# Three all-head attention stages: scores once with the mask added by VectorE, exponentials turned by TensorE, and VectorE's copies four banks behind its maxima

## What is computed

```
logits = q @ k.T * scale           # per head, 256 x 256
att    = softmax(where(mask, logits, -inf))
x      = x + (att @ v) @ Wo.T      # L3x: x + relu(...)
```

## Time and profile before

| | |
|---|---|
| median of 3 runs | 1761.01 us |
| profiled execution, its own time | 1761.7 us |
| its span | 1760.0 us |
| mean granted TensorE clock | 0.908 |
| busy: TensorE, VectorE, ScalarE, GpSimd | 1415.8, 875.7, 756.1, 430.4 us |
| L0a: start, 192 banks of exponentials, end | 29.1, 66.8 to 405.7, 415.6 us |
| L2a: start, 96 banks, end | 951.6, 992.2 to 1152.7, 1161.8 us |
| L3x: 128 banks | 1417 to 1625 us |

### The profile page before, as it was taken

How to read it: one execution, slowest core, us unless ns; L and a number is a source line. 1 busy time by engine, 2 the same in 40 slices (tenths; PEclk the granted TensorE clock), 3 DMA queues, 4 the chain that set the end, 5 groups by cost and what they waited for, 6 DMA issues and landing times. The chain is left out here.

```text
span 1760.0 us, 27583 instructions
## 1 busy us (share of the span) xinstructions
PE 1415.8 (80%) x10001; PEld 785.2 (45%) x10001; DVE 875.7 (50%) x2460; ACT 756.1 (43%) x1609; POOL 430.4 (24%) x513
## 2 busy tenths in 40 slices
PE   6899999997899999885997899976083577787585
PEld 4344444444544444463455344455062434444364
DVE  4555555542355555455213565447223657666433
ACT  3244443443177777451440133443020467776233
POOL 4533333310121110100001444201544042210134
PEclk9999999998999999895999999987586889999687
DMA  7900000000000000000003100000122000000022
GB/s 209 133 1 1 2 1 1 1 1 0 1 1 1 1 1 1 1 1 1 1 1 127 51 1 1 1 1 10 51 80 78 1 19 13 7 13 1 7 59 77
DMA packets 60255, 42.31 MB, mean 24 GB/s; under 512 B 13189, under 2 KB 54121, under 8 KB 60121
## 3 DMA queue, kind: packets, MB, share of 16 engines
q1 hardware_dynamic: 54752, 32.42, 7.7%
q0 software_dynamic: 3552, 7.33, 1.2%
q10 hardware_dynamic: 1816, 0.81, 0.2%
HBM read 25.88 MB, written 14.66 MB: 23 GB/s over the span
## 5 line engine op out<-in xcount | busy, mean ns | idle before, releaser
L885 ACT ACTIVATE L0a_probs<-L0a_psL 128x512 f32<-128x512 f32 x192 | 104.2, 594 | 202.0 <-PE L0a_psL L693 73.5
L1262 ACT ACTIVATE L3x_e<-L3x_e,L3x_neg_max 128x256 f32<-128x256 f32 x256 | 112.4, 499 | 55.8 <-DVE L3x_neg_max L1314 55.2
L949 DVE TENSOR_REDUCE L0a_mx_part<-L0a_psS 128x4 f32<-128x512 f32 x120 | 77.3, 686 | 105.6 <-PE L0a_psS L636 81.3
L1182 PE MATMUL L3x_psE<-ident,L3x_e 128*128 128x128 f32 x512 | 84.3, 297 | 38.6 <-ACT L3x_e L1262 25.1
L1314 DVE CUSTOM_DVE_ANT_0 L3x_e<-L3x_psS,L3x_mask_rows 128x256 f32<-128x256 f32 x256 | 93.5, 420 | 31.2 <-PE L3x_psS L1174 30.9
L538 POOL TENSOR_SCALAR L0a_km<-L0a_kT,quad_rows 128x256 f32<-128x256 f32 x64 | 58.4, 930 | 199.3 <-ACT L0a_kT L856 199.3
L628 PE MATMUL L0a_psS<-L0a_km,L0a_qT 32*128 32x512 f32 x360 | 101.4, 640 | 0.2 <-DVE L0a_mx_part L954 0.2
L885 ACT ACTIVATE L2a_probs<-L2a_psL 128x512 f32<-128x512 f32 x96 | 52.1, 595 | 107.3 <-PE L2a_psL L689 72.5
L1182 PEld LDWEIGHTS L3x_psE<-ident,L3x_e 128*128 128x128 f32 x512 | 58.6, 149 | 87.2 <-ACT L3x_e L1262 68.3
L662 PE MATMUL L0a_psL<-L0a_qm,L0a_kT 32*128 32x512 f32 x256 | 72.1, 637 | 21.8 <-DVE L0a_mx L949 20.3
L1516 PE MATMUL L1a_psL<-L1a_soft_near,neg_tri 128*128 128x512 f32 x128 | 67.9, 612 | 0.2 <-DVE L1a_soft_near L1723 0.2
(11 more groups left out here) (719 smaller groups left out, 3476.4 us busy)
## 6 DMA issues: line engine op xcount, KB each, us to landing
L2f_rows<-packed_rows SPq DMA_DIRECT2D x8, 325.0 KB
packed_rows<-zeros SPq DMA_DIRECT2D x1, 2560.0 KB, 32.4
experts_L_L<-in_L_ffn_w_dram SPq DMA_DIRECT2D x1, 2048.0 KB, 8.9
unpacked_rows<-zeros SPq DMA_DIRECT2D x1, 2048.0 KB, 22.5
scores_L_experts_L<-in_L_ffn_w_dram SPq DMA_DIRECT2D x1, 2048.0 KB, 8.0
L2f_back_rows<-unpacked_rows SPq DMA_DIRECT2D x16, 128.0 KB, 2.6
L3x_mask_rows<-in_mask_Bx1xSxS_ff_dram SPq DMA_DIRECT2D x8, 256.0 KB, 2.7
sorted_rows<-zeros SPq DMA_DIRECT2D x1, 1472.0 KB, 20.1
```

Source lines behind the costliest of these rows:

```text
L885: nc.scalar.activation(probs[:, half, a, k, :], psL[i % RING][:], ACT.Exp, scale=scale).then_inc(s_prob, 1)
L949: nc.vector.tensor_reduce(dst, psS[a][:].rearrange("p (j n) -> p j n", j=4), AX.X, ALU.max).then_inc(s_red, 1)
L1182: last = nc.tensor.transpose(psE[i % 2][:, c * P:(c + 1) * P], e[:, i % RING, c * P:(c + 1) * P], mem.ident[:])
L1262: last = nc.scalar.activation(at, at, ACT.Exp, bias=neg[:, i % RING, j:j + 1], scale=-1.0)
```

## The change

In `quad_heads` the second pass goes away: scores are computed once, with the query rows on the partitions, and handled as `masked_heads` handles them. `qm`, the maxima's way through TensorE, `shift`, `hide` and both mask matmuls are gone. `reduce` adds the mask (`causal_rows` is new, built by GpSimd in the prologue) and writes minima and shifted scores; in group 0 a bank has 4 pieces of 128 columns, in groups 1 and 2 it has 2 of 256. `exponent` has as many pieces. The projections' copies, the copy of `raw` and the norm change engines: `keep_h` and `keep_raw` go to VectorE, `next_h` and `divide` to GpSimd. In both functions `score` of the next group stands one bank earlier in TensorE's queue (r == 1), and VectorE's `keep` of a bank stands four banks behind its `reduce`; `settle_x` of batch b stands at the first bank of b + 2. In `masked_heads` ScalarE's `invert` and `keep_h` move by one bank.

```diff
 def quad_heads(...):
-                def variants(src, dst, b, done):
...
+                def next_h(b):
+                    if b == 0:
+                        pool.wait_ge(scales, 2)
+                    else:
+                        pool.wait_ge(s_turn, b)
...
+                next_h(0)
+                next_h(1)
                 nc.gpsimd.memset(v[:], 0.0).then_inc(consts, 1)
...
                 for b in range(NB):
+                    if b + 2 < NB:
+                        if rope:
+                            combine(b + 2)
+                        variants(b + 2)
+                    if biased:
+                        add_bias(b)
+                    if b > 0:
+                        divide(b - 1)
+                    if b + 4 < NB:
+                        next_h(b + 4)
...
+                def score(group):
+                    b, g = divmod(group, GROUPS)
+                    if group >= 1:
+                        pe.wait_ge(s_red, 4 * group)
...
+                def turn_exp(i):
+                    pe.wait_ge(s_exp, i + 1)
+                    if i >= 2:
+                        wait_kept(pe, i - 2)
...
+                    for c in range(4):
+                        last = nc.tensor.transpose(psE[i % 2][:, c * P:(c + 1) * P], e[:, i % RING, c * P:(c + 1) * P], mem.ident[:])
+                    last.then_inc(s_et, 1)
...
+                    for n in range(ITEMS):
+                        i = ITEMS * b + n
+                        g, r = divmod(n, 4)
+                        if r == 1 and i + 3 < LAST:
+                            score(i // 4 + 1)
+                        if n == 0 and b > 0:
+                            weigh(b - 1, 0)
+                            weigh(b - 1, 1)
+                        if n == 1 and b > 0:
+                            weigh(b - 1, 2)
+                        if n == 2 and b > 0:
+                            weigh(b - 1, 3)
+                        if n == 3 and b + 2 < NB:
+                            queries(b + 2)
+                        if n == 5 and b > 0:
+                            spread_sums(b - 1)
+                        if n == 5 and b + 2 < NB and rope:
+                            keys(b + 2)
+                        if n == 7 and b + 2 < NB:
+                            values(b + 2)
+                        if n == 10 and b > 0:
+                            project(b - 1)
+                        if n == 10 and b + 3 < NB:
+                            turn(b + 3)
+                        turn_exp(i)
...
+                for i in range(LAST):
+                    b, n = divmod(i, ITEMS)
+                    exponent(i)
+                    if i >= 2 and i % 2 == 0:
+                        keep(i - 2)
+                    if n == 3 and 2 <= b and b - 2 + B < NB:
+                        scale_rows(b - 2)
+                    if n == 5 and b + 2 < NB and not rope:
+                        keep_qk(b + 2)
+                    if n == 7 and b > 0:
+                        invert(b - 1)
...
+                dve.wait_ge(consts, 4)
...
+                    for j in range(pieces(i)):
+                        at = slice(j * n, (j + 1) * n)
+                        last = nc.vector.tensor_tensor_reduce(out=e[:, i % RING, at], in0=psS[r][:, at], in1=hidden, scale=-scale, scalar=MOST,
+                                                              op0=ALU.add, op1=ALU.min, accum_out=neg[:, i % RING, j:j + 1])
...
+                for i in range(LAST):
+                    b, n = divmod(i, ITEMS)
+                    reduce(i)
+                    if i % 2 == 1 and i >= 4:
+                        keep(i - 4)
+                    if n == 0 and b >= 2:
+                        settle_x(b - 2)
+                    if n == 2 and b + 2 < NB:
+                        keep_h(b + 2)
+                    if n == 6 and b > 0:
+                        keep_raw(b - 1)
+                    if n == 7 and b + 2 < NB and rope:
+                        rotate(b + 2)
+                    if n == 9 and b + 2 < NB and rope:
+                        rotate_keys(b + 2)
+                    if n == 11 and b + 2 < NB:
+                        keep_v(b + 2)
 def masked_heads(...):
-                        if r == 2 and i + 2 < LAST:
+                        if r == 1 and i + 3 < LAST:
                             score(i // 4 + 1)
...
-                    if n == 6 and b > 0:
+                    if n == 7 and b > 0:
                         invert(b - 1)
-                    if n == 9 and b + 2 < B:
+                    if n == 10 and b + 2 < B:
                         keep_h(b + 2)
...
-                    if n % 4 == 0 and i > 0:
-                        keep(i - 1)
-                    if n % 4 == 3:
-                        keep(i - 2)
-                    if n == 14 and b > 0:
-                        settle_x(b - 1)
+                    if i % 2 == 1 and i >= 4:
+                        keep(i - 4)
+                    if n == 0 and b >= 2:
+                        settle_x(b - 2)
```

More of the change, by code:

```diff
@@ L534, in _ @@
                     nc.gpsimd.memset(at[:, :, HD:VW], 1.0).then_inc(consts, 1)
[L536 to L563 removed]
+                for b in range(2):
+                    if rope:
+                        combine(b)
+                    variants(b)
+                    next_h(b + 2)
+                for b in range(NB):
+                    if b + 2 < NB:
+                        if rope:
+                            combine(b + 2)
+                        variants(b + 2)
+                    if biased:
+                        add_bias(b)
[3 more added lines that the diff above has]
+                        next_h(b + 4)
+                divide(NB - 1)
             @block.tensor
@@ L646, in first_scores @@
                     for r in range(4):
                         rows = slice(32 * r, 32 * r + 32)
-                        last = nc.tensor.matmul(first_banks[r][:], qT[rows, 0, t * P:(t + 1) * P], km[rows, 0, :, u * P:(u + 1) * P],
-                                                start=True, stop=hidden is None, skip_group_check=True)
-                        if hidden is None:
-                            last.then_inc(s_score, 1)
-                    if hidden is not None:
-                        for r in range(4):
-                            nc.tensor.matmul(first_banks[r][:], mem.identb[:], hidden.unsqueeze(1).to_broadcast([P, 4, P]), start=False,
-                                             stop=True, skip_group_check=True).then_inc(s_score, 1)
@@ L818, in _ @@
+                for r in range(4):
+                    weigh(NB - 1, r)
                 spread_sums(NB - 1)
@@ L969, in divide, with reduce @@
-                def divide(b):
-                    dve.wait_ge(s_rec, b + 1)
-                    nc.vector.tensor_tensor(yT[:], yT[:], raw[:], ALU.mult).then_inc(s_yT, 1)
+                def reduce(i):
+                    b, g, r = place(i)
+                    n = 512 // pieces(i)
+                    hidden = of(b).mask[:, 0, 0:P] if g == 0 else of(b).mask[:, 1, :]
+                    if i >= RING:
+                        dve.wait_ge(s_et, i - RING + 1)
+                    dve.wait_ge(s_score, i + 1)
+                    for j in range(pieces(i)):
+                        at = slice(j * n, (j + 1) * n)
+                        last = nc.vector.tensor_tensor_reduce(out=e[:, i % RING, at], in0=psS[r][:, at], in1=hidden, scale=-scale, scalar=MOST,
+                                                              op0=ALU.add, op1=ALU.min, accum_out=neg[:, i % RING, j:j + 1])
+                    last.then_inc(s_red, 1)
@@ L986, in settle_x @@
                     dve.sem_inc(s_bn, 1)
-                next_h(0)
                 for b in range(2):
-                    next_h(b + 1)
+                    keep_h(b)
                     if rope:
```

424 lines of the change are left out of this document (131 added, 293 removed).

## The result

The kernel after takes **1748.46 us** (median of 4 runs, 1748.13 to 1748.97) against 1761.59 for the kernel before beside it: ratio **0.9923**, 95% interval 0.9908 to 0.9938. The forecast was 1690 with a range of 1640 to 1740, so the direction was right and the time is outside the range. One of the four runs of the kernel before was a slow one (1795.89 us) and is left out of the ratio.

A forecast was written before the change was run, and what follows sets the result against it. TensorE's matmuls bound L0a and L2a; in L3x no engine was full and waits set the time. Gains 30 - 3 + 22 + 22 = 71 us from 1761.7 gave 1690, own range 1662 to 1716, wider range 1640 to 1740.

The forecast's parts named there:

- L0a's round 3: L0a, the round of the next batch's group 0: VectorE needs 7.0 us, TensorE is done by 6.2.
- L3x's round 4: Last of L3x's four rounds a batch: the second `weigh` waits for keep 13 behind `settle_x`; 6.6 us.
- the allowance for it (1.0 a batch): All three loops: 1.0 us added to every batch for TensorE running at L3x's clock of 0.94.
- L0a: L0a's loop: rounds 5.8, 5.5 and 7.0, a batch 19.3 us with the 1.0, against 21.2; 30 us gained.
- L2a: L2a's loop: rounds 5.8, 6.5 and 8.5, 21.8 us in five batches; loop 164 against 160.5, -3 us.
- the wait for `divide`: L2a's round 3: GpSimd's `divide` ends 4.0 us into the round, while TensorE reaches `project` at 1.7.
- L3x: L3x's loop: rounds 5.3, 5.5, 4.8 and 6.6, a batch 23.2 us against 26.0; 22 us gained.
- what it buys is the keep of four banks earlier: L3x: turns are done when VectorE comes to them; its 40.3 us of waits go, partly becoming waits for scores.
- Starts and ends: L0a and L2a: first exponentials 12.7 and 13.5 us earlier, ends -4; together 22 us gained.
- the wait for the clearing of `v`: L0a's start: VectorE copies batch 0 only after GpSimd's clearing, at 44.1 us, where ScalarE did it at 39.5.
- The rival "handoffs stay": Loops don't get shorter: L0a gains nothing, L2a loses 3, L3x gains 11, starts 22; 1731 us, chance 0.22.
- The slower rival: TensorE at its lower clock level: gains gone at a mean clock of 0.88, 1824 us at 0.80; chance 0.07.

The follow-up runs named there:

- e1: The changed kernel with `settle_x` one bank later, behind the second bank's reduce and keep, in all three stages: 1682.74 us, ratio 0.9542.
- e8: e1 with the next group's scores back at the third bank and VectorE's copies two banks behind: 1680.91 us on another chip, ratio 0.9703.
- e6: e1 and e3 together, plus `v` cleared before batch 1's norm and `keep(LAST - 3)` ahead of the last but one `settle_x`: 1620.73 us, ratio 0.9358.
- e3: The changed kernel with GpSimd's `divide` ahead of the masked keys, only in the stage with rotation (L2a): 1727.83 us, ratio 0.9791.
- e7: e1 with the next group's scores back at the third bank, copies still four banks behind: 1761.07 us on another chip, ratio 1.0162.

## Why the prediction was wrong

- **The failed step** is in L0a's round 3: "TensorE waits for keep 9 before the second `weigh`, and is done by 6.2", and its like in L3x's round 4. Keep 9 (keep 13 in L3x) is also what the turn of the last bank waits for, since both use one bank of `psE`. That turn stands ahead of *both* `weigh`s and was costed as done before. So the keep behind `settle_x` stops TensorE with a turn, two `weigh`s and another turn still to do, one after the other (196.69 to 199.27): 8.47 in place of 7.0.
- **What that makes in the prediction's own prices**: the turn (0.59) and the first `weigh` (0.70) come on top of 6.2, 7.5 in L0a; in L3x 0.59 and 0.93 on top of 6.6, 8.1, where 8.24 was measured at the upper clock. The other 1.0 in L0a is mostly VectorE, which starts keep 9 at 5.06 (190.80 to 195.86) where the sum had 4.24. `settle_x` waits 0.53 for `project`, a wait that was put at nothing though the sum's own prices have `project` end at 2.6 and `settle_x` start at 2.1; and there are 0.25 of idle time behind its statistics.
- **The clock** then adds 1.56 in half of L0a's rounds and 1.4 to 1.6 in five of six in L3x. In the loops of L0a and L3x the allowance for it (1.0 a batch) was thus not far off, though it was taken from "some 16 us" of TensorE work in L3x, where the earlier trace rows has 160.72 / 8 = 20.1. e1 takes away the wait behind the keep, the wait for `project` and with them the lower clock, and gives 66 us.
- **L0a**: 18.43 in e1, where the sum was 18.3 plus an allowance of 1.0. Most prices were right: 128 columns 0.21 apart on VectorE, a bank of four pieces 1.28 on ScalarE (1.2 taken), rounds 5.56 and 5.68 (5.8 and 5.5 forecast). With the waits and the lower clock the loop gained 19.1, not 30.
- **L2a**: the wait for `divide` was there as forecast (2.51 us, forecast 2.3), but round 3 was 11.8 to 14.0, not 8.5: `settle_x` in VectorE's queue waits for the late `project`, then the keep, then turn 11. Two waits that I had side by side are in series. The loop lost 20.6, not 3. With either one removed it is 20.35 or 22, with both 19.2.
- **L3x**: round 4 was 9.62 to 9.88, once 8.24, instead of 6.6, the other three 5.64, 5.77, 5.40 (5.3, 5.5, 4.8 forecast); 7.3 gained, not 22. The sentence "what it buys is the keep of four banks earlier" is not borne out: e8, with copies two banks behind and most of the waits for turns still there, has 23.98, nearly e1's 23.56. The kernel before already had the scores at the third bank; compared with it, e8 changes only the places of the keeps and of `settle_x`, and two of ScalarE's steps by one bank. Which of these gives the 2 us was not tested.
- **Starts and ends**: the wait for the clearing of `v` was forecast and is there; the starts gained 9.6 and 11.6 instead of 12.7 and 13.5, and in L2a the projection behind the idle time ran at the lower level. The ends cost 11.4 instead of 4: the last `settle_x` but one stands ahead of the last two keeps (TensorE waits 1.95 in L0a and 1.88 in L2a for the first of them), `project` waits 2.69 for GpSimd's `divide` (before, 2.08 for VectorE's), and in L0a, not in L2a, two of the last four `weigh`s take 1.10 and one 0.93 instead of 0.64. e6 has the keep first: 3.5 us less in L0a and 1.8 in L2a up to ScalarE's last instruction.
- **The rival "handoffs stay"** (1731) gave a time nearer to the result, by another mechanism: what stays is not the chain of single banks but one queue position. **The slower rival** had its break-even at a mean clock of 0.88 in the quad loops; L0a is at 0.95, L2a at 0.87. The turns are not what brought it down: e1 and e6 have the same turns and hold 0.99 in L0a and L3x. By the rule of the Trainium skill (TensorE: Matmul & The Clock Gate, Part 4: PE-mode transpose), that transposes don't count as activity as matmuls do, one would expect these loops to fall too; their traces don't bear that out. No run has a long stretch of transposes alone.

## What to carry to other kernels

When a copy frees a bank, list every instruction that waits for it and take the first in its engine's queue, not the one whose data it is; then ask what stands ahead of the copy in *its* queue, and move that behind it. The distance of a copy and the place of the next group's issue are one choice: in L0a two banks went with the late scores and four with the early ones (19.4 and 18.4 us a batch), and the mixed pairs took 21 and more; in L2a only the pair of e1 stood out. A forecast of a hand-written order should walk at least one batch with every wait of every engine; adding rounds up from prices alone came near e1's time (1690 against 1682.74), not that of the kernel. Part of that nearness is luck: e1's loop in L0a is 18 us shorter than the sum, and starts and ends gained less.

## What was not expected of the hardware

The same idle time of 2.61 us left TensorE at its higher level in one batch (0.63 for four transposes) and at the lower in the next (1.09), in alternation over most of L0a; the low rounds cost 1.56 us more. The alternation is not a rule. In e3's L2a the same turn waits 2.54 or 2.76 us in six batches, and TensorE comes out of four of these waits in a row at the higher level, out of the first and the last at the lower. Nor does it take a wait of this length: in e7 a turn at 115.55 runs mostly at the lower level (0.97) behind waits of 1.31 and 0.91 us. What decides it is open.

The turns, 48 transposes in a batch, hold a clock of 0.99 in e1 and e6, where no wait of TensorE in L0a's middle batches is longer than 1.0 us. Whether filling the idle stretch with other matmuls would keep the clock was not tried: each of the eight banks of PSUM that these stages hold has a use already.
